# Second attention, second pass: waits by half of the heads, values and group sums shared between two engines

## The chip, the cores and the metric

The kernel runs on one core of a Trainium2 chip, in one launch. The metric is the device time of the launch in microseconds (us). Before the change it is 1446.17 us, the median of three runs (1443.87 to 1449.4). "PE" is TensorE's matmuls, "PEld" its weight loads, "DVE" VectorE, "ACT" ScalarE, "POOL" GpSimd, "SPq" the queue from which SyncE issues transfers.

## What is computed

A Perceiver of depth 2: 128 latent tokens `x` (128 x 256) attend to a long context `ctx_768` (12544 x 192), then to themselves, then pass through a mixture of 8 experts, and all of this a second time with other weights. The change touches only the second cross attention:

```python
q = x @ Wq                      # 128 x 1024: 16 heads of 64
k = context @ Wk                # 12544 x 1024
v = context @ Wv
sim = jnp.einsum('bhid,bhjd->bhij', q, k) * SCALE
attn = jax.nn.softmax(sim, axis=-1)
out = jnp.einsum('bhij,bhjd->bhid', attn, v)
return out @ Wo + bo
```

## The kernel before

Every value that needs more than 16 bits of precision is held as a pair: a high part in fp16 and a low part, which is the rest in fp16. The second attention makes two passes over the context. The first makes the keys, writes them to DRAM and finds each head's maximum. The second, `attend1` in each engine's program, makes the values, the scores, the exponentials and the weighted sums. It takes the 16 heads in two groups `g` of 8, and in each group goes over the context in `NT` = 98 tiles of 128 rows: 196 tiles, numbered `i = g * NT + t`. The group switch is at tile 98.

TensorE's program in iteration `i` (all its matmuls are recorded at L847):

1. `value_products`: 5 matmuls of 512 columns give the values of tile `i` in one of two PSUM banks (`v_bank`). It waits until the values of tile `i-2` have been taken out.
2. `score1` for two halves `j` of 4 heads: 8 matmuls of 128 columns each, into one of three PSUM banks (`s_bank`). A half waits until the low part of the third half before it has been made (`low_made`).
3. `weigh1` for tile `i-1`: per head one matmul of 130 columns (high probabilities by high and low values) and one of 66 (low probabilities by high values), 16 in all, added up over the 98 tiles in three banks of three, three and two heads. Before the first of them it waits for the exponentials of both halves (`exped`), the tile's values (`values_made`) and the low parts of both halves (`low_made`).

ScalarE per tile: on odd tiles the copy of the values' high part (L1464), then for each half two exponentials of 128x512 (L1367), one to fp16 in SBUF and one in fp32 in place in PSUM.

VectorE per tile: on even tiles the copy of the values' high part (L1762), then the values' low part by a subtraction (L1587, `v<-ps,v`), then for each half the probabilities' low part by a subtraction (L1587, `p<-ps,p`), which raises `low_made`. In the first tiles one step of `maxima1(1)` stands behind each half: the maxima of the second group's heads, from which its softmax shifts are made. When they are there, TensorE turns them with two small matmuls at iteration 8 (`SECOND_SHIFT`), VectorE writes them beside the queries (`add_shifts`, L1587 `q_all<-ps,by`), and TensorE's scores of tile 8 wait for that. The queries that this writes are those of the second group.

At the group switch VectorE runs `normalise1(0)`: it waits for the last weighing of the first group and reads the three banks of sums straight from PSUM (scaling, copy L1789, addition), before it does anything for tile 98. TensorE's `weigh1` of tile 98 waits for these reads bank by bank, as its first matmul in a bank clears the old sums. `divide1`, the division for the first group, stands behind tile 101. At the end `normalise1(1)` does the same for the second group.

GpSimd clears a part of the keys' second buffer (L831) as soon as the second group's maxima are reduced. ScalarE loads its table of exponentials after its last copy of the first pass.

Of the kernel before, what the change touches and what calls it, by code (L numbers as in the profile page):

```python
# [9 lines left out]
ALU = mybir.AluOpType  # L10
# [3 lines left out]
P = 128  # L14
# [27 lines left out]
def perceiver_kernel(nc, d, out):  # L42
# [18 lines left out]
    with ExitStack() as ctx:  # L61
# [3 lines left out]
        def sem(name):  # L65
            return ctx.enter_context(nc.semaphore(name))
# [84 lines left out]
        values0_summed, values0_out = sem("values0_summed"), sem("values0_out")  # L151
        sums_read = sem("sums_read")
        scored, exped, low_made, weighed, att_made = (
# [272 lines left out]
        def v_bank(i):  # L426
            return ps[:, 3 + i % 2, 0:L1.gw]

        def n_scored1(g, t, j):
            return 2 * NT + (g * NT + t) * 2 + j + 1  # L430

        def out_cols(h):
# [412 lines left out]
        def tensor(pe):  # L845
# [220 lines left out]
            def weigh1(g, t):  # L1066
                i, b = g * NT + t, t % 2
                pe.wait_ge(exped, n_scored1(g, t, 1))
                pe.wait_ge(values_made, i + 1)
                pe.wait_ge(low_made, 2 * i + 2)  # L1070
                if t == 0 and g == 0:
                    pe.wait_ge(max_copied, len(N_COP))
                    pe.wait_ge(max_reduced, len(N_RED))
                v4 = v_tile(i)
                kw = dict(skip_group_check=True)
                for h in range(8):
                    if t == 0 and g and h % L1.per_bank == 0:
                        pe.wait_ge(sums_read, h // L1.per_bank + 1)
                    o = out_cols(h)
                    hh = slice(h % 4 * P, (h % 4 + 1) * P)  # L1080
                    mm(o, p_split(0, b, h // 4)[:, hh], v4[:, h, :], t == 0 and h % L1.per_bank == 0, False, **kw)
                    ins = mm(o[:, 0:L1.dh + 2], p_split(1, b, h // 4)[:, hh], v4[:, h, 0:L1.dh + 2], False,
                             t == NT - 1, **kw)
                ins.then_inc(weighed, 1)

            def attend1():
# [5 lines left out]
                for i in range(2 * NT + 1):  # L1092
                    g, t = i // NT, i % NT
                    if i < 2 * NT:
                        if i == 1:
                            pe.wait_ge(max_copied, len(N_COP))
                        if i >= 2:
                            pe.wait_ge(values_made, i - 1)
                        if i == SECOND_SHIFT:

                            pe.wait_ge(shift_made, 4)
                            pe.wait_ge(low_made, 2 * i - 2)
                            mm(ps[L1.shift_rows, 2 * i % 3, 0:P], shift_pair, ident[:, :], True,
                               True).then_inc(shift_turned, 1)
# [260 lines left out]
        def scalar(act):  # L1365
# [51 lines left out]
            def first_pass(L):  # L1417
                for i, (kind, n, h) in enumerate(TURNS[L.n]):
# [32 lines left out]
            def attend1():  # L1451
                first_pass(L1)
                load_exp_table()
                for n, value in enumerate(part_stores(L1, NCH - 1, 1)):
                    act.wait_ge(st_hi[n], value)
                    act.wait_ge(st_low[n], value)
                for g in range(2):
                    for t in range(NT):
                        i = g * NT + t
                        if i % 2:  # L1460
                            act.wait_ge(values_summed, i + 1)
# [4 lines left out]
                        for j in range(2):  # L1466
# [111 lines left out]
        def vector(dve):  # L1578
# [176 lines left out]
            def split_values1(i):  # L1755
                v4 = v_tile(i)
                vp = v_bank(i).rearrange("p (h c) -> p h c", h=8)
                if i % 2 == 0:
                    dve.wait_ge(values_summed, i + 1)
                    if i >= 2:  # L1760
                        dve.wait_ge(weighed, NT + i - 1)
                    dve.tensor_copy(v4[:, :, 0:L1.dh], vp).then_inc(values_hi, 1)  # L1762
                    dve.wait_ge(values_hi, i // 2 + 1)
                else:
                    dve.wait_ge(values_hi_act, i // 2 + 1)
                tt(v4[:, :, L1.dh + 2:L1.vw], vp, v4[:, :, 0:L1.dh], ALU.subtract).then_inc(values_made, 1)
# [11 lines left out]

            def normalise1(g):
                dh, vw, gw, per = L1.dh, L1.vw, L1.gw, L1.per_bank  # L1780
                inv = small[:, 224:232]
                dve.wait_ge(weighed, NT + (g + 1) * NT)
                for h0 in range(0, 8, per):
                    nh = min(per, 8 - h0)
                    o = ps[:, O1_BANK + h0 // per, 0:nh * vw].rearrange("p (h c) -> p h c", h=nh)
                    a = att[:, g * gw + h0 * dh:g * gw + (h0 + nh) * dh].rearrange("p (h c) -> p h c", h=nh)
# [3 lines left out]
                    if g:  # L1790
                        dve.reciprocal(i, i)
                        settle(tt(a, o[:, :, dh + 2:vw], a, ALU.add))
                        tt(a, a, bc(i, 2, [P, nh, dh]), ALU.mult).then_inc(att_parts, 1)
                    else:
                        tt(a, o[:, :, dh + 2:vw], a, ALU.add).then_inc(sums_read, 1)

            def divide1():

                inv = small[:, 224:232]
                dve.wait_ge(sums_read, 3)  # L1800
                settle(dve.reciprocal(inv, inv))
# [14 lines left out]
            def attend1():  # L1816
                first_pass(L1)
                second_maxima = maxima1(1)
                for g in range(2):
                    for t in range(NT):  # L1820
                        i = g * NT + t
                        if i == SECOND_SHIFT:
                            add_shifts(1, 2 * i % 3)
                        split_values1(i)
                        for j in range(2):
# [229 lines left out]
```

## Time and profile before

| | |
|---|---|
| median of three runs | 1446.17 us |
| the profiled execution | 1446.07 us |
| its span, first to last instruction | 1444.3 us |
| PE busy | 1360.1 us (94%) |
| VectorE busy | 1111.1 us (77%) |
| ScalarE busy | 1070.2 us (74%) |
| second pass of the second attention, first value matmul to last weighing | 834.8 to 1386.7 us of the span |

The second pass is 552 us, 38% of the span, and the same tile 196 times. So it is read at two scales: the length of a tile in an undisturbed stretch, and the places where the rhythm breaks: its first nine tiles, the group switch and the end. A row of the timeline gives the start, the duration, engine, line, operation and the tiles written and read; in square brackets stands how long the engine had been idle and what released it.

### The profile page before, as it was taken

What the parts mean: (1) busy time and instruction counts of PE and PEld (TensorE: products, weight loads), DVE (VectorE), ACT (ScalarE), POOL (GpSimd) and SP (SyncE); (2) the same over time, 40 slices, a digit from 0 to 9 for tenths busy, and PEclk for the clock granted to TensorE, in tenths of its full rate; (3) what the DMA queues carried; (4) which work ended last, traced back from release to release, by engine and by line L of the source; (5) the groups of instructions that cost most, each with busy time, mean ns of one, the idle gap of its engine ahead of it and who ended that gap; (6) DMA issues with size and microseconds to landing.
All of it is one profiled execution on the core that took longest, in us unless ns stands there. A gap on an engine that the chain in (4) does not pass through costs nothing.

```text
span 1444.3 us, 37910 instructions
## 1 busy us (share of the span) xinstructions
PE 1360.1 (94%) x15595; PEld 899.9 (62%) x15595; DVE 1111.1 (77%) x1678; ACT 1070.2 (74%) x1590; POOL 198.9 (14%) x196
## 2 busy tenths in 40 slices
PE   5888889999999999999999979999999999999989
PEld 2445456666777694333333357777777777777768
DVE  5677678998000777999999988888888888888864
ACT  3667665666997466888888868888888787888841
POOL 6333210000000006000000000000000004341630
PEclk9999999999999999999999999999999999999999
DMA  4457549564664574556655566788777689898910
GB/s 144 174 198 239 180 151 233 137 141 116 168 170 136 205 246 147 191 187 226 216 189 192 188 134 132 152 154 154 146 144 143 117 176 184 177 188 172 226 70 5
DMA packets 137138, 240.01 MB, mean 166 GB/s; under 512 B 10412, under 2 KB 120710, under 8 KB 136966
## 3 DMA queue, kind: packets, MB, share of 16 engines
q1 hardware_dynamic: 136966, 237.58, 62.4%
q8 instruction: 125, 2.05, 0.6%
q14 instruction: 47, 0.39, 0.1%
HBM read 159.30 MB, written 78.23 MB: 164 GB/s over the span
## 4 chain that ended last, share of the span: by engine, by line
PE 84%; DVE 8%; ACT 3%; issue 3%; POOL 1%; DMA 0%; SPq 0%; POOLq 0%; DVEq 0%; ACTq 0%
PE ps L847 83%; DVE W L1617 2%; ACT W L1391 2%; DVE W L1587 1%; DVE p L1587 1%; DVE q_all L1587 1%; DMA W<-in_ctx_dram 0%; PE ps L886 0%; ACT ps L1367 0%; DVE q_all L1915 0%; POOL q_all L767 0%; ACT p L1367 0%; DVE att L1587 0%; DVE v L1587 0%; DVE v L1762 0%
## 5 line engine op out<-in xcount | busy, mean ns | idle before, releaser
L1367 ACT ACTIVATE p<-ps 128x512 f16<-128x512 f32 (+1 forms) x490 | 329.3, 682 | 94.9 <-PE ps L847 93.7
L1587 DVE TENSOR_TENSOR p<-ps,p 128x512 f16<-128x512 f32 (+1 forms) x467 | 350.7, 752 | 61.9 <-ACT ps L1367 59.4
L847 PEld LDWEIGHTS ps<-q_all,W 128*128 128x128 f16 (+1 forms) x3544 | 230.4, 99 | 70.4 <-issue 5.6
L847 PE MATMUL ps<-q_all,W 128*128 128x128 f16 (+2 forms) x3544 | 265.3, 226 | 7.5 <-DVE p L1587 4.4
L1367 ACT ACTIVATE ps<-ps 128x512 f32<-128x512 f32 x392 | 235.8, 602 | 0.0
L847 PE MATMUL ps<-v,p 128*128 128x130 f16 x3136 | 169.8, 206 | 7.2 <-DVE p L1587 2.7
L847 PE MATMUL ps<-wv,ctxT_a_hi 128*128 128x512 f16 (+1 forms) x588 | 156.0, 347 | 12.8 <-DVE W L1617 10.0
L847 PEld LDWEIGHTS ps<-v,p 128*128 128x128 f16 x3136 | 147.5, 97 | 14.3 <-issue 4.8
L1587 DVE TENSOR_TENSOR v<-ps,v 128x512 f16<-128x512 f32 x196 | 135.4, 691 | 17.7 <-ACT v L1464 5.3
L847 PE MATMUL ps<-wv,ctxT_b 128*128 128x512 f16 (+1 forms) x504 | 137.0, 340 | 0.0
L1700 DVE TENSOR_REDUCE W<-ps 128x1 f32<-128x448 f32 x224 | 125.0, 616 | 11.5 <-PE ps L847 11.5
L847 PE MATMUL ps<-W,q_all 64*128 64x448 f16 (+2 forms) x620 | 126.3, 355 | 6.1 <-DVE ctxT_b L1639 2.3
L847 PE MATMUL ps<-ctxT_a_hi,q_all 128*128 128x512 f16 x448 | 122.5, 355 | 2.7 <-DVE p L1587 2.1
L847 PE MATMUL ps<-ctxT_b,q_all 128*128 128x512 f16 (+1 forms) x456 | 116.6, 357 | 0.0
L1367 ACT ACTIVATE W<-ps 128x1024 f32<-128x1024 f32 x98 | 95.1, 1023 | 26.5 <-PE ps L847 25.4
L1406 ACT CAST W<-ps 128x1344 f16<-128x1344 f32 (+1 forms) x81 | 102.5, 1265 | 2.7 <-PE ps L847 2.6
L847 PE MATMUL ps<-wv,ctxT_a_lo 128*128 128x512 f16 (+1 forms) x294 | 101.8, 346 | 0.0
L1393 ACT CAST p<-ps 128x896 f16<-128x896 f32 x75 | 68.0, 906 | 28.6 <-PE ps L847 28.1
L847 PE MATMUL ps<-ctxT_a_lo,q_all 128*128 128x512 f16 (+2 forms) x284 | 86.3, 336 | 0.8 <-DVE q_all L1587 0.8
L847 PEld LDWEIGHTS ps<-ctxT_a_hi,q_all 128*128 128x128 f16 x448 | 34.7, 97 | 70.6 <-issue 37.3
L1464 ACT CAST v<-ps 128x512 f16<-128x512 f32 x98 | 57.6, 588 | 26.3 <-PE ps L847 25.6
L1770 DVE COPY att<-ps 128x512 f32<-128x512 f32 x1 | 0.7, 691 | 97.8 <-PE ps L847 97.8
(279 smaller groups left out, 2037.9 us busy)
## 6 DMA issues: line engine op xcount, KB each, us to landing
W<-keys_hi SPq DMA_DIRECT2D x54, 896.0 KB, 8.2
W<-keys_low SPq DMA_DIRECT2D x27, 896.0 KB, 11.5
keys_hi<-p SPq DMA_DIRECT2D x75, 224.0 KB, 1.9
keys_low<-p SPq DMA_DIRECT2D x75, 224.0 KB, 1.9
keys_hi<-W SPq DMA_DIRECT2D x65, 224.0 KB, 2.1
keys_low<-W SPq DMA_DIRECT2D x65, 224.0 KB, 1.9
W<-values SPq DMA_DIRECT2D x28, 484.0 KB, 4.2
W<-in_L_ffn_W_dram SPq DMA_DIRECT2D x10, 1024.0 KB, 10.7
```

The source lines that it names most:

```text
L847: return pe.matmul(out_, lhsT, rhs, start=start, stop=stop, **kw)
L1367: return act.activation(out_, in_, ACT.Exp, scale=scale)
L1391: ins = act.activation(dst, src, ACT.Identity, bias=bk_scaled[:, i:i + 1])
L1393: ins = act.copy(dst, src)
L1406: act.copy(dst.rearrange("p (n k) -> p n k", n=banks), src).then_inc(max_copied, 1)
L1464: act.copy(v_tile(i)[:, :, 0:L1.dh], v_bank(i).rearrange("p (h c) -> p h c", h=8)).then_inc(values_hi_act, 1)
L1587: return dve.tensor_tensor(out_, a, b, op)
L1617: ins = dve.scalar_tensor_tensor(out=low, in0=src, scalar=bk_scaled[:, i:i + 1], in1=hi, op0=ALU.add, op1=ALU.subtract)
L1700: dve.tensor_reduce(late_parts[:, h - G0, k:k + 1], ps[:, LATE_BANKS[j % 3], 0:MAXC], AX.X, ALU.max).then_inc(late_reduced, 1)
L1770: dve.tensor_copy(att[:, 512:1024], ps[:, O0_BANK, :]).then_inc(outT_made, 1)
```

## The change

- `weigh1` no longer waits for `exped`, nor for both halves' low parts ahead: it waits for half 0's before its first head and for half 1's before its fifth.
- The copy of the values' high part is ScalarE's on tiles 0 to 7 and 98 too, besides the odd ones (`act_copies`); VectorE has the rest.
- The reading of the first group's sums: the three banks are copied as they are to SBUF (`RAW1`), the first and third by VectorE (`read_sums1`, behind half 0 and half 1 of tile 98), the second by ScalarE behind its exponentials of tile 98. High and low sums are added from these copies in SBUF, one bank behind each of the tiles 99, 100, 101, and divided behind tile 102 (`divide1`, now a generator). `normalise1` is the second group's alone and as it was.
- The turn of the second group's shifts stands in iteration 8 behind the scores, before the weighing of tile 7, and waits for the low parts of tile 7; the wait for the finished rows moves from the scores of tile 8 to those of tile 9.
- The table of exponentials is loaded ahead of the last copy of the first pass instead of behind it.

```diff
@@ tensor, weigh1
                 i, b = g * NT + t, t % 2
-                pe.wait_ge(exped, n_scored1(g, t, 1))
                 pe.wait_ge(values_made, i + 1)
-                pe.wait_ge(low_made, 2 * i + 2)
...
                 for h in range(8):
+                    if h % 4 == 0:
+                        pe.wait_ge(low_made, 2 * i + h // 4 + 1)
                     if t == 0 and g and h % L1.per_bank == 0:
-                        pe.wait_ge(sums_read, h // L1.per_bank + 1)
+                        pe.wait_ge(*((sums_read, 1), (sums_copied, 1), (sums_read, 2))[h // L1.per_bank])
@@ tensor, attend1
-                        if i == SECOND_SHIFT:
-
-                            pe.wait_ge(shift_made, 4)
-                            pe.wait_ge(low_made, 2 * i - 2)
-                            mm(ps[L1.shift_rows, 2 * i % 3, 0:P], shift_pair, ident[:, :], True,
-                               True).then_inc(shift_turned, 1)
...
-                        if i == SECOND_SHIFT:
+                        if i == SECOND_SHIFT + 1:
                             pe.wait_ge(rows_made, 4)
...
+                    if i == SECOND_SHIFT:
+
+                        pe.wait_ge(shift_made, 4)
+                        pe.wait_ge(low_made, 2 * i)
+                        mm(ps[L1.shift_rows, (2 * i - 1) % 3, 0:P], shift_pair, ident[:, :], True,
+                           True).then_inc(shift_turned, 1)
                     if i:
                         weigh1((i - 1) // NT, (i - 1) % NT)
@@ scalar, first_pass and attend1
                     elif kind == "max" and not is_direct(L, h):
+                        if L is L1 and i == len(TURNS[1]) - 2:
+                            load_exp_table()
                         copy_maxima(L, n, h, PAIR[L.n][i])
...
-                        if i % 2:
+                        if act_copies(i):
                             act.wait_ge(values_summed, i + 1)
...
+                        if i == NT:
+                            act.wait_ge(weighed, 2 * NT)
+                            act.copy(sums_of(1, RAW1[1]), sums_of(1, ps[:, O1_BANK + 1, :])).then_inc(sums_copied, 1)
@@ helpers, new
+        def act_copies(i):
+            return i % 2 == 1 or i < SECOND_SHIFT or i == NT
@@ vector, new or changed
+            def read_sums1(b):
+                dve.wait_ge(weighed, 2 * NT)
+                dve.tensor_copy(sums_of(b, RAW1[b]), sums_of(b, ps[:, O1_BANK + b, :])).then_inc(sums_read, 1)
...
             def divide1():
-                dve.wait_ge(sums_read, 3)
+                dve.wait_ge(sums_read, 2)
+                dve.wait_ge(sums_copied, 1)
+                for b in range(3):
+                    h0, o = b * per, sums_of(b, RAW1[b])
+                    nh = o.shape[1]
+                    ts(inv[:, h0:h0 + nh], o[:, :, dh], VS, None, ALU.mult)
+                    tt(att[:, h0 * dh:(h0 + nh) * dh].rearrange("p (h c) -> p h c", h=nh), o[:, :, dh + 2:vw],
+                       o[:, :, 0:dh], ALU.add).then_inc(sums_added, 1)
+                    yield
+                dve.wait_ge(sums_added, 3)
                 settle(dve.reciprocal(inv, inv))
...
                         for j in range(2):
...
                             next(second_maxima, None)
-                        if i == NT + 3:
-                            divide1()
-                    normalise1(g)
+                            if i == NT:
+                                read_sums1(2 * j)
+                        if i > NT:
+                            next(first_sums, None)
+                normalise1()
```

## Rows read from the trace of the kernel before

**Rows 1.** The page: TensorE's busy time, share of the span, instructions.

```profile
PE 1360.1 (94%) x15595; PEld 899.9 (62%) x15595; DVE 1111.1 (77%) x1678; ACT 1070.2 (74%) x1590; POOL 198.9 (14%) x196
```

**Rows 2.** Busy time by stretch: bounds, length, engines, granted clock, DMA share, GB/s.

```profile
841.35:870.55 29.20, 24.40 (x298) 17.67 (x299) 24.89 (x40) 17.82 (x35) 3.08 (x1) 0.94 0.76 145
870.55:1112.34 241.79, 241.50 (x3297) 185.76 (x3294) 206.56 (x311) 207.28 (x401) 0.00 (x0) 1.00 0.75 144
1112.34:1133.36 21.02, 17.92 (x225) 13.61 (x223) 17.19 (x33) 13.99 (x28) 0.00 (x0) 0.92 0.65 126
1133.36:1383.13 249.77, 247.07 (x3370) 190.04 (x3368) 211.58 (x319) 212.27 (x411) 87.03 (x45) 1.00 0.85 178
```

**Rows 3.** Timeline of two tiles (96 and 97) of an undisturbed stretch.

```profile
1106.92 0.86 PE L847 MATMUL ps<-v,p 128*128 128x130 f16 x16
1107.62 0.59 PE L847 MATMUL ps<-wv,ctxT_a_hi 128*128 128x512 f16 x2
...
1108.69 1.06 PE L847 MATMUL ps<-q_all,W 128*128 128x128 f16 x16
1108.89 0.59 ACT L1464 CAST v<-ps 128x512 f16<-128x512 f32 x1 [0.21 <-PE ps L847]
...
1109.59 0.86 PE L847 MATMUL ps<-v,p 128*128 128x130 f16 x16
...
1110.86 0.61 ACT L1367 ACTIVATE ps<-ps 128x512 f32<-128x512 f32 x1
...
1111.36 1.06 PE L847 MATMUL ps<-q_all,W 128*128 128x128 f16 x16
1111.50 0.69 DVE L1587 TENSOR_TENSOR p<-ps,p 128x512 f16<-128x512 f32 x1 [0.31 <-ACT ps L1367]
...
1112.31 0.74 PEld L847 LDWEIGHTS ps<-v,p 128*128 128x128 f16 x16
1112.34 0.86 PE L847 MATMUL ps<-v,p 128*128 128x130 f16 x16
```

**Rows 4.** TensorE's weight loads, waits from 1133.36 to 1383.13: total, times, longest.

```profile
PEld ps L847 <- issue: 3.5, 5, 1.3
```

**Rows 5.** Timeline of the first tiles of the second pass.

```profile
834.92 1.28 ACT L1406 CAST att<-ps 128x1344 f16<-128x1344 f32 x1 [1.75 <-PE ps L847]
...
836.22 1.28 ACT L1367 ACT_TABLE_LOAD   x1
...
837.51 0.20 ACT L1367 ACTIVATE small<-minus_half 128x1 f32<-128x1 f32 x1
...
841.35 0.86 PE L847 MATMUL ps<-v,p 128*128 128x130 f16 x16 [1.26 <-ACT ps L1367]
...
847.83 3.08 POOL L831 MEMSET W<- 64x3584 f32 x1 [151.28 <-DVE small L1725]
...
848.54 2.40 DVE L1584 TENSOR_SCALAR small<-small 128x8 f32<-128x8 f32 x1
...
852.32 0.62 PE L847 MATMUL ps<-q_all,W 128*128 128x128 f16 x8 [1.36 <-DVE p L1587]
```

**Rows 6.** Timeline at iteration 8, the second group's shifts.

```profile
865.66 1.22 DVE L1587 TENSOR_TENSOR q_all<-ps,by 32x1024 f16<-32x1024 f32 x1
...
866.94 1.07 PE L847 MATMUL ps<-q_all,W 128*128 128x128 f16 x16 [1.50 <-DVE q_all L1587]
```

**Rows 7.** Timeline of the group switch.

```profile
1117.34 1.03 PE L847 MATMUL ps<-q_all,W 128*128 128x128 f16 x8 [2.62 <-DVE p L1587]
...
1118.17 1.51 PE L847 MATMUL ps<-v,p 128*128 128x130 f16 x16
...
1119.49 0.92 PE L847 MATMUL ps<-wv,ctxT_a_hi 128*128 128x512 f16 x2
```

**Rows 8.** The page's groups: busy time, mean ns of one, idle time before, releaser.

```profile
L847 PEld LDWEIGHTS ps<-v,p 128*128 128x128 f16 x3136 | 147.5, 97 | 14.3 <-issue 4.8
...
L1770 DVE COPY att<-ps 128x512 f32<-128x512 f32 x1 | 0.7, 691 | 97.8 <-PE ps L847 97.8
```

More of the change, by code:

```diff
@@ L151, in perceiver_kernel @@
         values0_summed, values0_out = sem("values0_summed"), sem("values0_out")
-        sums_read = sem("sums_read")
+        sums_read, sums_copied, sums_added = sem("sums_read"), sem("sums_copied"), sem("sums_added")
         scored, exped, low_made, weighed, att_made = (
@@ L427, in v_bank, with n_copies, sums_of @@
             return ps[:, 3 + i % 2, 0:L1.gw]
+        def act_copies(i):
+            return i % 2 == 1 or i < SECOND_SHIFT or i == NT
+        def n_copies(i):
+            by_act = sum(act_copies(k) for k in range(i + 1))
+            return by_act if act_copies(i) else i + 1 - by_act
         def n_scored1(g, t, j):
             return 2 * NT + (g * NT + t) * 2 + j + 1
+        RAW1 = W[:, 14864:15254], W[:, 15254:15644], att[:, 512:772]
+        def sums_of(b, region):
+            nh = min(L1.per_bank, 8 - b * L1.per_bank)
+            return region[:, 0:nh * L1.vw].rearrange("p (h c) -> p h c", h=nh)
         def out_cols(h):
@@ L1452, in attend1 @@
                 first_pass(L1)
-                load_exp_table()
                 for n, value in enumerate(part_stores(L1, NCH - 1, 1)):
@@ L1757, in split_values1 @@
                 vp = v_bank(i).rearrange("p (h c) -> p h c", h=8)
-                if i % 2 == 0:
+                if act_copies(i):
+                    dve.wait_ge(values_hi_act, n_copies(i))
+                else:
                     dve.wait_ge(values_summed, i + 1)
-                    if i >= 2:
-                        dve.wait_ge(weighed, NT + i - 1)
+                    dve.wait_ge(weighed, NT + i - 1)
                     dve.tensor_copy(v4[:, :, 0:L1.dh], vp).then_inc(values_hi, 1)
-                    dve.wait_ge(values_hi, i // 2 + 1)
-                else:
-                    dve.wait_ge(values_hi_act, i // 2 + 1)
+                    dve.wait_ge(values_hi, n_copies(i))
                 tt(v4[:, :, L1.dh + 2:L1.vw], vp, v4[:, :, 0:L1.dh], ALU.subtract).then_inc(values_made, 1)
@@ L1777, in normalise0, with normalise1 @@
                    ALU.mult).then_inc(att_made, 1)
-            def normalise1(g):
+            def normalise1():
                 dh, vw, gw, per = L1.dh, L1.vw, L1.gw, L1.per_bank
                 inv = small[:, 224:232]
[L1782 to L1786, printed above, removed]
+                dve.wait_ge(weighed, 3 * NT)
+                for b in range(3):
+                    h0 = b * per
+                    o = sums_of(b, ps[:, O1_BANK + b, :])
+                    nh = o.shape[1]
+                    a = att[:, gw + h0 * dh:gw + (h0 + nh) * dh].rearrange("p (h c) -> p h c", h=nh)
                     i = inv[:, h0:h0 + nh]
@@ L1789, in normalise1 @@
                     settle(dve.tensor_copy(a, o[:, :, 0:dh]))
[L1790 to L1795, printed above, removed]
+                    dve.reciprocal(i, i)
+                    settle(tt(a, o[:, :, dh + 2:vw], a, ALU.add))
+                    tt(a, a, bc(i, 2, [P, nh, dh]), ALU.mult).then_inc(att_parts, 1)
+            def read_sums1(b):
+                dve.wait_ge(weighed, 2 * NT)
+                dve.tensor_copy(sums_of(b, RAW1[b]), sums_of(b, ps[:, O1_BANK + b, :])).then_inc(sums_read, 1)
             def divide1():
+                dh, vw, per = L1.dh, L1.vw, L1.per_bank
                 inv = small[:, 224:232]
-                dve.wait_ge(sums_read, 3)
+                dve.wait_ge(sums_read, 2)
+                dve.wait_ge(sums_copied, 1)
+                for b in range(3):
+                    h0, o = b * per, sums_of(b, RAW1[b])
+                    nh = o.shape[1]
+                    ts(inv[:, h0:h0 + nh], o[:, :, dh], VS, None, ALU.mult)
[3 more added lines that the diff above has]
+                dve.wait_ge(sums_added, 3)
                 settle(dve.reciprocal(inv, inv))
@@ L1817, in attend1 @@
                 first_pass(L1)
-                second_maxima = maxima1(1)
+                second_maxima, first_sums = maxima1(1), divide1()
                 for g in range(2):
@@ L1822, in attend1 @@
                         if i == SECOND_SHIFT:
-                            add_shifts(1, 2 * i % 3)
+                            add_shifts(1, (2 * i - 1) % 3)
                         split_values1(i)
```

## The prediction, made before the changed kernel was run

> **What bounds the kernel now.** I read the page first: PE is busy 94% of the span [rows 1], so only PE's gaps and its waits inside the rhythm can give time back. Then the second pass by stretches [rows 2], cut where a weighing starts: tiles 0 to 8, 8 to 97, 97 to 103, 103 to 194. By length: 29.20/8 = 3.65 us a tile, 241.79/89 = 2.717, 21.02/6 = 3.50, 249.77/91 = 2.745. Two stretches are slow by about 25%, and there the granted clock is 0.94 and 0.92 as well. Last, the timelines of single tiles, to see what releases PE.
>
> In the even stretch PE looks 99.9% busy, but the intervals between weighings alternate: 1109.59 - 1106.92 = 2.67 us and 1112.34 - 1109.59 = 2.75 [rows 3]. The parts tell why. Weighing to values is 0.70, values to scores 1.07 in both. Scores to weighing is 0.90 in one (1108.69 to 1109.59) and 0.98 in the other (1111.36 to 1112.34), though the 16 matmuls are the same. In the second, VectorE's low part ends at 1111.50 + 0.69 = 1112.19, and the weight load starts 0.12 later: PE waits for `low_made`. The loop behind it runs over two tiles, from one odd weighing to the next: weighing 0.70, values 1.07, then 0.20 to ScalarE's copy at 1108.89, 1.97 to its last exponential at 1110.86, 0.64 to VectorE's low part, 0.69 for it, 0.15 to the matmul: 5.42 = 1112.34 - 1106.92. PE's own work for two tiles is 2 x 2.67 = 5.34. So a latency loop, not PE, sets the rhythm, by 0.08 us a pair.
>
> **The change part by part.** The sum is made against the profiled 1446.07 us (span 1444.3 and 1.8 around it); the median is 1446.17, 0.1 more.
>
> *Waits by halves.* The loop's last link is needed 0.35 us later (half of the 0.70). It becomes 5.42 - 0.35 = 5.07, under PE's 5.34, with 0.27 to spare. What else could be late at 2.67 a tile? ScalarE has 207.28 us busy in 241.79 and VectorE 206.56 [rows 2]: 2.33 and 2.32 a tile. So PE's work sets the rhythm and each pair gives 0.08: (89 + 91)/2 = 90 pairs, 7.2 us. Check: 241.79 - 89 x 2.67 = 4.2, and 249.77 - 91 x 2.67 = 6.8, of which 3.5 are stalls named "issue", where PE waits for nothing the trace shows [rows 4]; they stay. The added wait stands in front of the fifth head, and behind it in PE's queue are 8 matmuls, the next values and scores. Does a wait that is already met cost anything in the middle of a group? The scores have one before their ninth matmul and still take 0.90 for 16. The weighing of tile 98 has two such waits (for the sums) and takes 1119.49 - 1118.17 = 1.32 at the low clock, no more than twice 0.70 [rows 7]. I take 0; from below it can't be less, from above 0.10 a tile, about a quarter more than the 0.08 by which a late release delays it in rows 3.
>
> *Start, tiles 0 to 8.* The table load with its small exponential takes 1.28 + 0.20 = 1.48; the last copy has 1.75 idle ahead of it [rows 5], so in its new place it is hidden. Yet it frees little: the first exponential began at about 837.6, when the first scores were there anyway. Worth 0 to 0.1; I take 0. The Trainium skill (ScalarE: Activation LUTs, What ACT_TABLE_LOAD costs) puts a switch at 1.28 us and a drain of 1.38 behind it. The trace disagrees: the load ends at 837.50 and the next instruction starts at 837.51 [rows 5]. By the skill's figure the load would delay the last copy by 1.1 us and the sum would be up to 1.1 higher.
> Tiles 0 to 3 are bound by VectorE: its maxima steps stand between the halves, and its 128x8 scaling takes 2.40 us beside GpSimd's 3.08 us clearing, both ending at 850.9 [rows 5]. That pair is triggered by the maxima and stays. The copy of values on tile 0 was in idle time; that of tile 2 (0.7) stood ahead of the reductions that start the clearing, so clearing and scaling end 0.7 earlier, at about 850.2. The weighing by halves gives 0.35 more, once, since the next wait is VectorE's again. Worked through tile by tile, the weighing of tile 3 ends near 853.0 instead of 854.2: 1.2 us. The copies of tiles 4 and 6 fall where VectorE idles. ScalarE has with every copy 0.5 + 2.1 = 2.6 us a tile, just under 2.67: no gain, no loss. The clock loss in this stretch is 6% of 29.20, 1.75 us; PE's idle shares before it are nearly as before (one gap grows from 1.4 to 1.9, the others shrink), so I leave it; if it goes, 1.6 more are won.
> *Shift rows.* Before, PE idled 1.50 before the scores of tile 8 while VectorE wrote the rows for 1.22 [rows 6]; counted from start to start of its work it lost 1.7. Now scores come first and the turned shifts behind them. But VectorE has more behind them: rows 1.22, then tile 8's high copy, value low and half 0's low part, back to back about 2.0 (0.69 is one alone [rows 3]), and PE needs that last one for the second half of tile 9's scores. From the end S of tile 8's scores: PE turns the shifts for 0.4, weighs 0.70, makes values 1.07 and the first half of scores 0.45, and wants it at S + 2.6. VectorE starts at S + 0.6 and ends at S + 3.85. So the stall doesn't go, it moves one tile on and measures about 1.3 instead of 1.6: 0.3 won. Bounds: 0, and all of 1.7. With 0.2 from two pairs of the loop, the start gives 1.2 + 0.3 + 0.2 = 1.7 us.
>
> *Group switch.* 21.02 - 6 x 2.67 = 5.0 us are lost now: VectorE's nine operations on the sums stand ahead of tile 98's work, PE idles 2.62 [rows 7], the clock falls (8% of 21.02 = 1.7 us), and the division costs the rest. New, from the end S of tile 98's scores: weighing 97 to S + 0.70; half 0's low part to S + 1.6; VectorE copies 390 columns, by the 0.69 for 512 [rows 8] about 0.54, to 2.2; half 1's low part to 2.9; 260 columns to 3.3. ScalarE's exponentials end at 1.9, its copy at 2.4. PE weighs 98 from S + 2.66, head 3 needs 2.4, head 4 needs 2.99 and comes at 3.0, head 6 needs 3.42 and comes at 3.18: 0.25 idle. Then VectorE carries 0.5 us of additions on each of tiles 99 to 101 and 0.9 on 102, while it has 0.3 a tile to spare; on 101, 103 and 104 the second half of the scores waits some 0.37 each. Total 0.25 + 1.1 = 1.35 idle, too spread out to bring the clock down. Gain 5.0 - 1.35 = 3.65 us; bounds 1.5 (the clock falls all the same, and half a us more) to 5.0.
>
> *End.* The last weighing's first half runs before its wait: 0.35, as only 8 matmuls are left behind the last low part. Gain 0.3.
>
> Sum: 7.2 + 1.7 + 3.65 + 0.3 = 12.85. 1446.1 - 12.8 = 1433.3 us, 0.9% faster. Its own range is 1429 to 1437.
>
> **The rivals.** What a run can tell from no change is 0.5%, 7.2 us, so faster means under 1438.9 and slower over 1453.4.
>
> (a) *The rhythm stays.* The 0.08 comes from elsewhere, or VectorE or ScalarE drifts late in the tighter loop. For it: half 1's low part will be seen only 0.27 before it is needed. Against it: the sum of the loop meets 5.42 exactly. Then 7.2 fall away: 1440.5. Chance 0.12.
>
> (b) *The sums only change places.* VectorE's added work at the switch (390 and 260 columns, additions, division) brings PE's clock down again and the stall back; 3.65 fall away: 1437. Chance 0.08.
>
> (c) *Slower: the wait in mid-group breaks the flow of weight loads.* TensorE's loads run ahead of its matmuls; if the fifth head's can't before the wait is read, each of 196 weighings has a bubble. It decides from 12.8/196 = 0.065 us a tile. At 0.10, a whole load laid bare (97 ns [rows 8]), it is 19.6 us: 1453, slower than before if not measurably. Against it: the scores' mid-group wait. The Trainium skill (TensorE: Matmul & The Clock Gate, Part 2) says that loads are pulled ahead of matmuls in flight, and names no wait as a limit; no row here shows a wait inside a weighing at the full clock. Chance 0.06.
>
> **How the numbers follow.** Forecast 0.74, (a) 0.12, (b) 0.08, (c) 0.06. Range 1429 to 1441: down to the case in which the start's clock loss goes as well and stalls are smaller, up to (a). Faster: the forecast, (b) in most cases and a little of (a): 0.82. Same: most of (a), half of (c): 0.14. Slower: 0.04.
>
> **What would show it.** Intervals between weighings all 2.67 in the even stretches, no alternation, weight loads no longer 0.12 behind a low part. The clearing at about 847.1, and its end with the scaling at 850.2. No idle time before tile 8's scores but some 1.3 before the second half of tile 9's. Around the switch the clock at 1.00 and no idle time over 0.5. Wrong would be: alternation kept; a gap inside the weighing at head 4; a fallen clock at the switch.

## The result, and the profile after

The changed kernel takes 1428.05 us, the median of four runs (1427.46 to 1429.01); the kernel before took 1445.75 us in the same session (1443.87 to 1449.4). The ratio is 0.986 with a 95% interval of 0.985 to 0.988: 1.4% faster. 1433.3 us were predicted, with a range of 1429 to 1441; the time lies just under it.

The profiled execution took 1428.51 us, its span is 1426.8. The page gives the busy times, to be held against [rows 1]:

```profile
PE 1349.3 (95%) x15595; PEld 896.8 (63%) x15595; DVE 1106.5 (78%) x1672; ACT 1073.0 (75%) x1596; POOL 198.5 (14%) x196
```

TensorE executes as many instructions as before, in a span 17.5 us shorter. Where the time came from is seen in the same four stretches as in [rows 2], again cut where the weighings of tiles 0, 8, 97, 103 and 194 start; the fifth row begins at the first value matmul of the pass:

```profile
839.67:866.94 27.27, 23.01 (x301) 16.89 (x299) 23.99 (x38) 21.46 (x42) 3.08 (x1) 1.00 0.85 162
866.94:1104.78 237.84, 237.80 (x3297) 185.11 (x3294) 206.75 (x313) 206.89 (x400) 0.00 (x0) 1.00 0.77 146
1104.78:1121.05 16.27, 16.20 (x226) 12.48 (x224) 15.29 (x31) 14.34 (x29) 0.00 (x0) 1.00 0.84 164
1121.05:1365.98 244.93, 243.30 (x3370) 189.14 (x3368) 211.82 (x320) 212.28 (x411) 85.89 (x43) 1.00 0.87 182
...
834.20:866.94 32.74, 28.48 (x342) 20.29 (x341) 28.26 (x43) 25.79 (x50) 3.08 (x1) 0.96 0.76 146
```

For the kernel before, that fifth stretch reads:

```profile
834.78:870.55 35.77, 29.70 (x342) 20.70 (x341) 30.86 (x48) 24.23 (x45) 3.08 (x1) 0.92 0.70 134
```

| stretch | before | after | gain | predicted |
|---|---|---|---|---|
| up to the first value matmul of the pass | 834.78 | 834.20 | 0.58 | 0 |
| from there to weighing 8 | 35.77 | 32.74 | 3.03 | 1.7 |
| weighing 8 to 97 | 241.79 | 237.84 | 3.95 | 3.6 |
| 97 to 103, the group switch | 21.02 | 16.27 | 4.75 | 3.65 |
| 103 to 194 | 249.77 | 244.93 | 4.84 | 3.6 |
| the last tiles | | | 0.4 | 0.3 |

**The rhythm.** Three weighings in a row, to be held against [rows 3]:

```profile
1098.55 1.06 PE L863 MATMUL ps<-q_all,W 128*128 128x128 f16 x16
...
1099.44 0.86 PE L863 MATMUL ps<-v,p 128*128 128x130 f16 x16
...
1102.11 0.86 PE L863 MATMUL ps<-v,p 128*128 128x130 f16 x16
...
1103.88 1.06 PE L863 MATMUL ps<-q_all,W 128*128 128x128 f16 x16
1104.02 0.69 DVE L1607 TENSOR_TENSOR p<-ps,p 128x512 f16<-128x512 f32 x1 [0.31 <-ACT ps L1383]
...
1104.78 0.86 PE L863 MATMUL ps<-v,p 128*128 128x130 f16 x16
```

1102.11 - 1099.44 and 1104.78 - 1102.11 are both 2.67: the alternation is gone. Scores to weighing is now 0.90 in the odd tile too (1103.88 to 1104.78). VectorE's low part ends at 1104.71, only 0.07 ahead of the weighing's start; before, the weight load came 0.12 behind it and the matmul 0.15. Now the first head doesn't need it, the fifth does. From weighing 8 to 97, 88 of 89 intervals are 2.67, and in the last stretch 89 of 91; the three others hold a stall.

**The start**, to be held against [rows 5, 6]:

```profile
832.97 1.28 ACT L1383 ACT_TABLE_LOAD   x1
834.26 0.20 ACT L1383 ACTIVATE small<-minus_half 128x1 f32<-128x1 f32 x1
834.37 1.26 ACT L1422 CAST att<-ps 128x1344 f16<-128x1344 f32 x1
...
846.84 3.08 POOL L847 MEMSET W<- 64x3584 f32 x1 [150.47 <-DVE small L1745]
847.55 2.40 DVE L1604 TENSOR_SCALAR small<-small 128x8 f32<-128x8 f32 x1
851.33 0.62 PE L863 MATMUL ps<-q_all,W 128*128 128x128 f16 x8 [1.77 <-DVE p L1607]
...
863.16 1.22 DVE L1607 TENSOR_TENSOR q_all<-ps,by 32x1024 f16<-32x1024 f32 x1 [0.60 <-PE ps L863]
866.49 0.62 PE L863 MATMUL ps<-q_all,W 128*128 128x128 f16 x8 [1.03 <-DVE p L1607]
```

The pair of clearing and scaling comes about 1 us earlier, 0.58 of it because the whole pass starts earlier, and is as long as before (3.08 and 2.40). The stall of the shifts has moved on to the second half of tile 9's scores and measures 1.03 instead of 1.50.

**The switch**, to be held against [rows 7]:

```profile
1106.30 0.56 DVE L1817 COPY W<-ps 128x390 f32<-128x390 f32 x1
1106.57 0.51 ACT L1492 COPY W<-ps 128x390 f32<-128x390 f32 x1
1107.37 0.42 DVE L1817 COPY att<-ps 128x260 f32<-128x260 f32 x1
1107.45 0.86 PE L863 MATMUL ps<-v,p 128*128 128x130 f16 x16
...
1110.18 0.16 DVE L1603 TENSOR_SCALAR small<-W 128x3 f32<-128x3 f32 x1
1110.25 0.35 DVE L1607 TENSOR_TENSOR att<-W 128x192 f32<-128x192 f32 x1
1110.52 0.68 DVE L1783 CAST v<-ps 128x512 f16<-128x512 f32 x1
```

Weighing 98 starts 2.67 behind weighing 97 (1107.45 - 1104.78), where 2.62 of idle time stood before. The six tiles take 16.27, against 6 x 2.67 = 16.02. The 0.25 between them is one wait, ahead of the second half of tile 101's scores:

```profile
1112.58 0.45 PEld L863 LDWEIGHTS ps<-q_all,W 128*128 128x128 f16 x8 [0.25 <-DVE p L1607]
```

**Stalls named "issue"** in weight loads from 1121.05 to 1365.98 (total, times, longest), against 3.5 in [rows 4]:

```profile
PEld ps L863 <- issue: 2.3, 2, 1.6
```

### The profile page after: what moved, and what is told of

The parts are those of the page before. It is cut to its first block, busy times and chain, and to the rows that moved or that the text cites. A ratio compares the mean times of both kernels' runs of the same rounds, so it can differ in the third digit from the quotient of the medians.

```text
span 1426.8 us, 37912 instructions
## 1 busy us (share of the span) xinstructions
PE 1349.3 (95%) x15595; PEld 896.8 (63%) x15595; DVE 1106.5 (78%) x1672; ACT 1073.0 (75%) x1596; POOL 198.5 (14%) x196
## 4 chain that ended last, share of the span: by engine, by line
PE 85%; DVE 7%; ACT 3%; issue 3%; POOL 1%; DMA 0%; SPq 0%; POOLq 0%; DVEq 0%; ACTq 0%
PE ps L863 84%; DVE W L1637 2%; ACT W L1407 2%; DVE W L1607 1%; DVE p L1607 1%; DVE q_all L1607 1%; DMA W<-in_ctx_dram 0%; PE ps L902 0%; DVE q_all L1949 0%; POOL q_all L783 0%; ACT p L1383 0%; ACT ps L1383 0%; DVE small L1604 0%; DVE v L1607 0%; DVE small L1944 0%
## 5 line engine op out<-in xcount | busy, mean ns | idle before, releaser
L1481 ACT CAST v<-ps 128x512 f16<-128x512 f32 x103 | 60.5, 587 | 19.5 <-PE ps L863 7.1
```

The costliest lines, as they stand in the source:

```text
L1481: act.copy(v_tile(i)[:, :, 0:L1.dh], v_bank(i).rearrange("p (h c) -> p h c", h=8)).then_inc(values_hi_act, 1)
```

## The experiments

All kernels were read in the same stretches; the table holds what the windows of each profile give. "V" is the first value matmul of the pass, "w8" the start of weighing 8, the clock is that of V to w8, "issue" the stalls of w103 to w194 that the profile puts down to no releaser. Each row is one profiled execution. The times of "clearing later", "`exped` kept", "two waits fewer", "old place of shifts", "no early copies" and "table last" have intervals that overlap that of the changed kernel, so what is said of their parts rests on these stretches.

| kernel | V to w8 | clock | w8 to w97 | w97 to w103 | w103 to w194 | issue |
|---|---|---|---|---|---|---|
| before | 35.77 | 0.92 | 241.79 | 21.02 | 249.77 | 3.5 |
| after | 32.74 | 0.96 | 237.84 | 16.27 | 244.93 | 2.3 |
| after, again | 32.75 | 0.96 | 237.63 | 16.26 | 245.75 | 2.7 |
| halves only | 33.83 | 0.97 | 237.63 | 19.47 | 244.39 | 1.7 |
| all but halves | 32.40 | 1.00 | 241.53 | 16.54 | 250.03 | 3.7 |
| old switch | 32.55 | 0.96 | 237.64 | 21.12 | 244.66 | 2.0 |
| waits at every head | 31.75 | 1.00 | 240.02 | 18.61 | 245.37 | 0.7, and 1.8 more |
| clearing later | 28.80 | 1.00 | 237.77 | 16.27 | 245.80 | 3.1 |
| `exped` kept | 31.66 | 1.00 | 237.78 | 16.27 | 244.27 | 1.1 |
| two waits fewer | 31.63 | 1.00 | 237.63 | 16.26 | 242.97 | none |
| both joined | 29.67 | 0.96 | 237.62 | 16.28 | 242.96 | none |
| old place of shifts | 32.15 | 1.00 | 237.62 | 16.27 | 246.31 | 3.3 |
| no early copies | 33.15 | 1.00 | 237.62 | 16.28 | 244.40 | 1.7 |
| table last | 32.91 | 1.00 | 237.77 | 16.28 | 244.65 | 2.0 |

**Halves only.** The kernel before, with only the waits of `weigh1` changed.

```diff
-                pe.wait_ge(exped, n_scored1(g, t, 1))
-                pe.wait_ge(low_made, 2 * i + 2)
...
                 for h in range(8):
+                    if h % 4 == 0:
+                        pe.wait_ge(low_made, 2 * i + h // 4 + 1)
```

> The kernel before with one edit: the weighing waits for the low parts half by half and no longer for the exponentials. Theory (a latency loop of 5.42 us over two tiles sets the rhythm, and its last link is now needed 0.35 us later): intervals between weighings 2.67 us throughout instead of 2.67 and 2.75 in turn, 0.08 x 90 pairs = 7.2 us, and some 0.4 at the end and up to 0.6 in the first tiles: about 1437.5 us. The losses at the group switch (5.0) and of the clock stay. Rival (ScalarE's and VectorE's lighter work on other tiles, or the sums' copies, made the rhythm even): the alternation stays and the time is 1445.

1432.48 us (1430.61 to 1439.44), ratio 0.990 (0.988 to 0.992). That is 5 us less than expected. All undisturbed intervals are 2.67. This one edit brings 4.16 + 5.38 = 9.5 us in the even stretches, of which 7.2 are the rhythm and the rest are fewer stalls; another 1.98 lie ahead of the pass (832.80 against 834.78), where nothing was edited. The switch is shorter too, with VectorE's old work still in it, as the clock held in this execution:

```profile
1104.26:1123.73 19.47, 16.36 (x225) 12.47 (x223) 17.13 (x33) 14.13 (x28) 0.00 (x0) 1.00 0.71 138
```

**All but halves**, the reverse: the changed kernel with the three old waits.

> The changed kernel with the waits of the weighing as before (exponentials, values and both halves' low parts ahead of the first head); the rest of the change stays. Theory: the 7.2 us of the rhythm and 0.4 of the end come back, alternation 2.67 and 2.75: about 1436 us. Rival: the other parts account for most of the gain and it stays under 1432.

1439.97 us (1438.55 to 1442.75), ratio 0.995 (0.993 to 0.996). The alternation is back, 2.66 and 2.76 in turn:

```profile
1000.54 0.86 PE L863 MATMUL ps<-v,p 128*128 128x130 f16 x16
...
1003.20 0.86 PE L863 MATMUL ps<-v,p 128*128 128x130 f16 x16
...
1005.96 0.86 PE L863 MATMUL ps<-v,p 128*128 128x130 f16 x16
```

So the halves are worth 3.7 + 5.1 in the even stretches, and rival (a) falls from both sides. In the start they give 0.75 (32.40 against 31.65 in other kernels at the full clock). The switch takes 16.54 without them: nearly all of its gain comes from the copies.

**Old switch.** The changed kernel with VectorE's nine operations on the sums back in their old place (`normalise1(0)`, and `divide1` behind tile 101); ScalarE's copy of sums goes, and the copy of tile 98's values is VectorE's again.

```diff
-                        pe.wait_ge(*((sums_read, 1), (sums_copied, 1), (sums_read, 2))[h // L1.per_bank])
+                        pe.wait_ge(sums_read, h // L1.per_bank + 1)
...
-                            if i == NT:
-                                read_sums1(2 * j)
+                    normalise1(g)
```

> The changed kernel with the group switch as before: VectorE reads the three banks of sums ahead of tile 98 and divides behind tile 101, and its copy of tile 98's values is its own again. Theory: six tiles from weighing 97 to 103 take 21.0 us again instead of 16.3, so 1432.8 us, of which 1.7 is the clock's fall (granted clock about 0.92 in that stretch). Rival (the switch's loss was mostly in the waits of the whole weighing, now gone by halves): under 18.5 us in that stretch and under 1430.5.

1434.41 us (1433.29 to 1437.01), ratio 0.991 (0.989 to 0.993). Its switch is as long as before, and the clock fell:

```profile
1105.26:1126.38 21.12, 18.01 (x226) 13.40 (x224) 17.17 (x33) 14.14 (x28) 0.00 (x0) 0.92 0.64 126
```

In this stretch its program is that of "halves only", whose switch took 19.47 at 1.00 with the same 3.1 us in which PE isn't busy (19.47 - 16.36 and 21.12 - 18.01). So of the 4.85 us that the old switch costs (21.12 - 16.27), 3.2 are idle time (19.47 - 16.27) and 1.65 the clock's fall, which came in two of the three profiles with the old switch. Rival (b) falls: with the copies the clock is 1.00 in all eleven profiles, and the stretch 16.3 in nine of them.

**Waits at every head.** Eight more waits on a value long reached, in each of 196 weighings: rival (c), enlarged.

```diff
                 for h in range(8):
+                    pe.wait_ge(values_made, i + 1)
```

> The changed kernel with one more wait ahead of each of the 8 heads of every weighing, all on the tile's values, which are made by then: 1568 waits that are met. Theory: a wait that is met costs TensorE nothing even in the middle of a group, 1428 us, weighing to values 0.70 us. Rival (a wait holds back the next weight load): at 10 ns each it is 15.7 us, 1444 us; at 50 ns 78 us, over 1500.

1433.75 us (1429.05 to 1439.29), ratio 0.991 (0.989 to 0.993). An undisturbed tile still takes 2.67 (of 180 intervals 173), as here with eight more waits inside the weighing:

```profile
1008.15 0.86 PE L863 MATMUL ps<-v,p 128*128 128x130 f16 x16
...
1010.82 0.86 PE L863 MATMUL ps<-v,p 128*128 128x130 f16 x16
```

So a wait already met costs nothing in the rhythm, and rival (c) falls. But the kernel is slower than the changed one (0.9885 to 0.9926 against 0.9848 to 0.9877), and there are more and longer stalls: the three stretches from w8 to w194 hold 504.0 us instead of 499.0, and one stall takes 2.4 at the switch. The profile names no releaser for them, but for one of 1.8 in the last stretch, which it puts down to the tile's values, for which the first head had already waited.

**The changed kernel again**, unedited, beside the next three.

> The changed kernel as it is, run beside the next ones. 1428 us; the issue stalls between tiles 103 and 194 about 2 us, as in its first profile.

1428.97 us (1427.91 to 1430.74), ratio 0.987 (0.985 to 0.989). The rhythm repeats to 0.2 us in 238; the stalls of the last stretch don't quite: 2.7 instead of 2.3.

**The clearing later.** GpSimd waits until the second group's shifts have been made, and ScalarE copies tile 8's values too.

```diff
-            pool.wait_ge(maxima_made, 4)
+            pool.wait_ge(shift_made, 4)
...
-            return i % 2 == 1 or i < SECOND_SHIFT or i == NT
+            return i % 2 == 1 or i < SECOND_SHIFT + 1 or i == NT
```

> The changed kernel with two edits: GpSimd clears its part of the keys' buffer after the shifts are made instead of beside their scaling, and ScalarE copies the high values of tile 8 too. Theory (VectorE's 2.40 us scaling of 128x8 waits for GpSimd, and the moved shift rows only moved the stall to tile 9 behind VectorE's work): the scaling takes about 0.16 us, TensorE's 1.8 us of idle time in tile 4's scores falls under 0.3, and its 1.0 in tile 9's scores to about 0.4; 2.5 us together, 1425.5 us. Rival (the scaling is slow by itself, or VectorE's maxima steps bind anyway): the first gap stays over 1.5 and the time within 0.7 of the changed kernel.

1427.04 us (1422.72 to 1428.47), ratio 0.985 (0.983 to 0.988). V to w8 takes 28.80; three kernels that change nothing in the start but TensorE's met waits, and had the full clock in it, took 31.63 to 31.75, so 2.9 are won: 2.1 between weighings 2 and 4 and 0.7 between 7 and 8.

```profile
847.64 0.17 DVE L1604 TENSOR_SCALAR small<-small 128x8 f32<-128x8 f32 x1
...
849.61 3.08 POOL L847 MEMSET W<- 64x3584 f32 x1 [151.83 <-DVE small L1607]
...
863.74 0.62 PE L863 MATMUL ps<-q_all,W 128*128 128x128 f16 x8 [0.31 <-DVE p L1607]
```

The same scaling takes 0.17 where it took 2.40 beside the clearing: 2.2 us of VectorE's time, and 2.1 of the tiles', were two engines in each other's way. The Trainium skill (SBUF — State Buffer, SBUF: two separate sides) says that VectorE, in some of its operations, and GpSimd take a common pair of ports in turns, each for a whole instruction. In the changed kernel's trace the scaling does end right behind the clearing (846.84 + 3.08 = 849.92, 847.55 + 2.40 = 849.95), which agrees in the main. The stall of tile 9 shrinks from 1.03 to 0.31 with tile 8's copy gone from VectorE.

**`exped` kept.** One more wait at the head of each weighing, as before the change; in the even stretches it is met some 0.7 us before (VectorE's low part, which needs the same exponentials, starts at 1104.02, the weighing at 1104.78).

```diff
+                pe.wait_ge(exped, n_scored1(g, t, 1))
                 pe.wait_ge(values_made, i + 1)
```

> The changed kernel with the wait for both halves' exponentials back ahead of the weighing (met some 0.7 us before it is reached), the low parts still half by half. Theory 1 (the issue stalls shrank because TensorE no longer stands at a wait and its queue runs ahead): rhythm 2.67, stalls as in the changed kernel, 1428 us. Theory 2 (they shrank because one instruction fewer stands ahead of each weighing): the stalls of the kernel before, 3.3 us between tiles 103 and 194 and 0.5 before, come back: 1430 us. Rival (the wait for the exponentials, not for the low parts, held the rhythm): alternation 2.67 and 2.75 again, 1435 us.

1427.15 us (1425.67 to 1428.02), ratio 0.986 (0.983 to 0.988). The rhythm is 2.67: the halves of `low_made` do it, not the missing wait. And the stalls fall to 1.1, although there is one wait more per tile.

**Two waits fewer.** Neither `weigh1` nor the value products wait for `values_made`; both are implied by the low parts they wait for anyway.

```diff
-                pe.wait_ge(values_made, i + 1)
...
-                        if i >= 2:
-                            pe.wait_ge(values_made, i - 1)
```

> The changed kernel without TensorE's two waits for values_made in each tile, which the waits for the low parts imply, since VectorE makes a tile's values before its low parts. Theory 1 (run-ahead): rhythm 2.67, 1428 us or up to 1 less. Theory 2 (fewer instructions): issue stalls under 1 us, 1426.5 us. Rival (each met wait leaves a bubble hidden in the 2.67): rhythm 2.63 or less, 1420 us.

1426.26 us (1425.37 to 1426.81), ratio 0.985 (0.983 to 0.988), below all runs of the unedited kernel beside it. w103 to w194 takes 242.97 = 91 x 2.67, to the hundredth, without a stall. That fits the theory that fewer instructions make fewer stalls, which "`exped` kept" with its 1.1 doesn't.

**Both joined:** the clearing later and two waits fewer.

> The changed kernel with both improvements: GpSimd's clearing after the shifts are made and tile 8's high copy on ScalarE, and TensorE without its two implied waits for values_made. If the gains add: start 28.8 us instead of 32.7, no issue stalls in the second long stretch (2 to 2.8 less), about 1422.5 us. Rival (the issue stalls land where they will): 1425.

1423.28 us (1421.99 to 1423.5), ratio 0.983 (0.982 to 0.985): the fastest version, 4.8 us below the median of the changed kernel, 0.3% by their ratios to the kernel before. Its last stretch has no stall either:

```profile
1116.60:1359.56 242.96, 242.96 (x3370) 189.25 (x3368) 212.00 (x320) 212.29 (x411) 85.99 (x44) 1.00 0.87 183
```

PE is busy for the whole of it: nothing is left there but its own work.

**The old place of the shifts.** The turn ahead of tile 8's scores, the wait for the rows too.

```diff
                         if i >= 2:
                             pe.wait_ge(values_made, i - 1)
+                        if i == SECOND_SHIFT:
+                            pe.wait_ge(shift_made, 4)
+                            pe.wait_ge(low_made, 2 * i - 2)
+                            mm(ps[L1.shift_rows, 2 * i % 3, 0:P], shift_pair, ident[:, :], True,
...
-                        if i == SECOND_SHIFT + 1:
+                        if i == SECOND_SHIFT:
...
```

> The changed kernel with the turn of the shift rows back ahead of tile 8's scores, and the wait for them too. Theory (the stall only moved one tile on, behind VectorE's work): the gap of 1.5 ahead of tile 8's scores returns, that of 1.0 in tile 9's goes, 0.3 to 0.6 us more in the first nine tiles: 1428.9 us. Rival (the move itself won the 1.7): 1430.3.

1429.16 us (1424.8 to 1431.42), ratio 0.987 (0.985 to 0.989). The old stall is back and tile 9's is gone; V to w8 grows by 0.5 at the same clock (32.15 against 31.65):

```profile
865.11 1.07 PE L863 MATMUL ps<-q_all,W 128*128 128x128 f16 x16 [1.53 <-DVE q_all L1607]
```

**No early copies on ScalarE:** tiles 0, 2, 4 and 6 are VectorE's again.

```diff
-            return i % 2 == 1 or i < SECOND_SHIFT or i == NT
+            return i % 2 == 1 or i == NT
...
-                    dve.wait_ge(weighed, NT + i - 1)
+                    if i >= 2:
+                        dve.wait_ge(weighed, NT + i - 1)
```

> The changed kernel with VectorE copying the values of tiles 0, 2, 4 and 6 again. Theory (only tile 2's copy stands ahead of the clearing): clearing 0.7 later, weighing 3 some 0.7 later, 0.8 us more without a fall of the clock, 1429.3 us; if the clock falls in that stretch, 1.6 more. Rival (ScalarE's copies cost as much there as they free): 1428.5.

1431.25 us (1429.6 to 1432.93), ratio 0.989 (0.987 to 0.991). V to w8 is 33.15 at the full clock, 1.5 more than 31.65 where 0.8 was expected, 0.7 of it ahead of weighing 0. VectorE's rows there:

```profile
837.42 0.86 DVE L1607 TENSOR_TENSOR W<-W,att 128x1344 f16<-128x1344 f16 x1
...
838.19 0.69 DVE L1784 CAST v<-ps 128x512 f16<-128x512 f32 x1
838.91 0.69 DVE L1607 TENSOR_TENSOR v<-ps,v 128x512 f16<-128x512 f32 x1
839.52 0.68 DVE L1607 TENSOR_TENSOR p<-ps,p 128x512 f16<-128x512 f32 x1
```

The copy follows VectorE's last work of the first pass without a gap, and the low parts follow the copy: it is not in idle time, it is a link of VectorE's chain.

**The table last:** loaded behind the last copy of the first pass, as before.

```diff
-                        if L is L1 and i == len(TURNS[1]) - 2:
-                            load_exp_table()
...
                 first_pass(L1)
+                load_exp_table()
```

> The changed kernel with the table of exponentials loaded behind the last copy of the first pass, as before. With ScalarE's copy of tile 0's values now behind the load too: copy at 837.7 instead of 836.6 after the first value matmul at 834.2, first exponential 0.3 to 0.6 later, the first tiles VectorE-bound, 0.5 us more: 1429 us. Rival (all of it is hidden): 1428.5.

1429.44 us (1426.49 to 1431.47), ratio 0.988 (0.986 to 0.990). V to w8 is 32.91, 1.25 more than 31.65 where 0.5 was expected, all of it ahead of weighing 0:

```profile
837.05 1.28 ACT L1383 ACT_TABLE_LOAD   x1
...
838.35 0.20 ACT L1383 ACTIVATE small<-minus_half 128x1 f32<-128x1 f32 x1
...
838.46 0.57 ACT L1480 CAST v<-ps 128x512 f16<-128x512 f32 x1
```

Now ScalarE has tile 0's copy to make behind the load, and VectorE waits for it. Without either edit the start is about 33.3: "halves only" has 33.83, of which 0.5 is the old place of the shifts. This is an estimate, as no run undoes these two edits alone, and as "halves only" had a low clock ahead of weighing 0; that is taken to cost nothing there, because its first exponential (835.76) comes 0.24 behind the end of the table load, with the small one between. With one of the edits undone the start takes 33.15 or 32.91, with both in place 31.65: alone they are worth some 0.2 and 0.4, together 1.7. Most of the gain needs both.

## Why the prediction was right or wrong

**Right: what bounds the even stretches, and which edit moves it.** A loop of 5.42 us over two tiles stood against 5.34 of PE's own work; it became shorter than PE's work and each pair gave 0.08. "Halves only" and "all but halves" show that this edit does it alone, "`exped` kept" that it is the wait for the low parts. 7.2 us were predicted for it; w8 to w97 gave 3.95 for 3.6.

**Right: a wait already met costs nothing in the rhythm** (waits at every head), and two mechanisms of the start: the pair of clearing and scaling stays and comes earlier, and the shifts' stall moves one tile on, with 1.03 where 1.3 was worked out; that gave 0.5 where 0.3 was predicted. The end gave 0.4 for 0.3.

**Failed: "3.5 are stalls named issue ...; they stay".** They did not. w103 to w194 had 6.8 over 91 x 2.67 and has 2.0; the rhythm's share is 3.6, so 1.2 came from these stalls. The two profiles with the old waits had 3.5 and 3.7 there, every one with the halves 3.3 or less, and with two waits fewer there was none. Whether this edit made the 1.2 is open: one and the same TensorE program gave 1.7 to 3.1 in five profiles. The number of instructions or waits alone does not order the runs: one more wait per tile gave 1.1, eight more gave 2.5 here and 5 us more in all.

What they wait for the traces show in part. Besides the kernel's transfers they hold packets of 16 KB on a queue that the profile calls "instruction" (q8), 55 of them from w8 to w194, one in some 9 us; 54 with two waits fewer, 57 with eight more. There are 26 stalls of matmuls named "issue" in these stretches, in twelve profiles, and every one ends 1.3 to 1.8 us behind the end of such a packet, and so do the two put down to values. In the changed kernel a packet stands from 1205.60 to 1206.99, and the longest stall ends at 1208.71:

```profile
q8 instruction: 1, 0.02, 5.8%
...
1206.81 0.42 PE L863 MATMUL ps<-v,p 128*128 128x130 f16 x6
1208.71 0.61 PE L863 MATMUL ps<-v,p 128*128 128x130 f16 x10 [1.48 <-issue]
```

That points to TensorE waiting for its own program. It is argued from the times alone, as no run changes the loading by itself, and why some packets come late is open.

**Failed: the size of the switch, 1.35 us left.** 0.25 were left. The copies cost what was priced (0.56, 0.51 and 0.42 for about 0.54, 0.5 and 0.4), but each step of additions occupies VectorE from 1110.18 to 1110.52, 0.34 instead of 0.5. With 0.3 a tile to spare it is nearly hidden: of the three predicted waits, on tiles 101, 103 and 104 with some 0.37 each, only that on 101 comes, with 0.25. The 0.25 inside weighing 98 doesn't come: the copy of 260 columns ends at 1107.79, 3.01 behind the end of tile 98's scores, where 3.3 was worked out, and weighing 98 keeps to its 2.67. That what is left equals this 0.25 is chance.

**Failed: the start's clock loss "left in".** The prediction left in 1.75 for a fall of the clock between weighings 0 and 8 and named 1.6 for the case that it goes. It went. The kernel before has the clock at its lower level, 1.2 GHz, in two stretches of the start, and weighing 3 stands in the second:

```profile
833.45:836.86 3.41, 3.41 (x11) 0.96 (x12) 3.08 (x4) 1.92 (x2) 0.00 (x0) 0.50 0.21 74
853.93:857.34 3.41, 3.41 (x22) 2.04 (x20) 1.99 (x4) 0.72 (x2) 0.00 (x0) 0.50 0.36 71
...
853.36 1.00 PE L847 MATMUL ps<-v,p 128*128 128x130 f16 x16 [0.42 <-DVE p L1587]
...
857.69 0.86 PE L847 MATMUL ps<-v,p 128*128 128x130 f16 x16
```

From weighing 3 to 4 it takes 4.33 (857.69 - 853.36), "all but halves" with the same waits takes 2.67: this fall cost 1.66. No other profile has it, "halves only" neither; whether the change or the execution took it away is open. The changed kernel has one fall, ahead of weighing 0:

```profile
833.70:837.12 3.42, 3.42 (x17) 1.55 (x14) 2.85 (x4) 2.41 (x4) 0.00 (x0) 0.50 0.20 72
```

It takes 5.47 from V to weighing 0, and 4.36 in "clearing later", which has the same program up to there and held the full clock. So this fall belongs to the execution and costs 1.1. The first fall of the kernel before stands in the same place, but there ScalarE was loading its table, and the first exponential waited for that; by "halves only" it is taken to have cost nothing. That makes 1.66 - 1.09 = 0.57 of the 3.03 the clock's.

**Failed: the schedule of the start, 1.7.** By the same reckoning it gave the rest, some 2.5 (3.03 - 0.57), an estimate. Undone one at a time at the full clock, the halves cost 0.75, the new place of the shifts 0.5, and the table's place or the copies 1.25 or 1.5, which comes to 2.5 to 2.75. Tile 0's copy and the table's load were each priced at nothing, on the ground that one was in idle time and the other hidden. Undone one at a time they cost 1.5 (with tiles 2 to 6) and 1.25, and most of that is not visible if the other is missing. Their rows were read as if each edit were made alone, and what each is worth shows only beside the other.

The Trainium skill puts a drain of about 1.38 us behind a table load (ScalarE: Activation LUTs, What ACT_TABLE_LOAD costs). By that figure, as an estimate, the last copy would have started at 835.63. It starts at 834.37, 0.12 behind the load's end with the small exponential between them, and in "table last" the next instruction follows the load by 0.02 as well; here the measurement decides.

A reading of the prediction is off as well: its first and third stretch are called slow by about 25%, but 3.65 and 3.50 us a tile are 34% and 29% above 2.717. Nothing else was worked out from that.

0.58 us lie ahead of the pass, where nothing was changed; this point moved between 832.80 and 836.54 over all profiles. The misses, 0.58 + 1.33 + 0.35 + 1.10 + 1.24 + 0.1, all have the same sign and make 4.7 us. The range had been taken from the rivals' side; towards the fast side it reached only to 4.3 below the forecast, though three disturbances of the kernel before (the clock losses of two stretches and the stalls) could each shrink. The time lies 0.95 under the range, so it took all of 1.33, 1.24 and 1.10 together: without any one of them it would have been inside.

## What to carry to other kernels

When an engine looks 99.9% busy, look at the intervals of single iterations: an alternation of 2.67 and 2.75 held 7.2 of the 8.8 us won in the even stretches, and it went with one wait set in front of the first operation that needs it. Work that two engines share at a start can't be priced edit by edit; write each engine's chain to the first result with all edits in place. And before shortening an operation that looks slow beside another engine's, ask what starts that other one: moving GpSimd's clearing, which PE did not wait for here, won some 2.1 us.

## What the runs showed of the hardware that was not expected

- A scaling of 128x8 on VectorE takes 0.17 us alone and 2.40 beside a 3.08 us clearing on GpSimd.
- PE's stalls without a real releaser (single ones of up to 2.6 us) differ with the waits in its program: 3.5 and 3.7 us from w103 to w194 with the old waits, 1.1 to 3.3 with the halves, none in both kernels with two waits fewer. 1568 waits more, all met, left each tile's 2.67 as it was and added 5 us of such stalls. All 26 that are named "issue" end 1.3 to 1.8 us behind a 16 KB packet of the "instruction" queue.
- The granted clock at the old group switch, with 3.1 us without PE in it each time, was 0.92 in two profiles and 1.00 in one; the fall is worth 1.65 us. From V to weighing 0 the same program had 0.73 or 1.00, which is 1.1 us.
- Another fall cost 1.66 us where PE was bound by its own work (weighing 3 to 4 before). One that stood where the next step waited for ScalarE's table load is taken to have cost nothing ("halves only").
